# Shared turns of three heads' outputs, and every second mask block copied by ScalarE

## The reference, cut to what matters

```python
Q, K, V = (...)                                # 16 heads of 8 columns each
scores = jnp.einsum('bhqd,bhkd->bhqk', Q, K) / scale
mask = _tpms_mask(L, phase, threshold, temperature)       # one 512 x 512 mask for each head
scores = scores + TPMS_WEIGHT * jnp.log(mask + 1e-06)[None]
attn = jax.nn.softmax(scores, axis=-1)
out = jnp.einsum('bhqk,bhkd->bhqd', attn, V)
out = out.transpose(0, 2, 1, 3).reshape(B, L, H)
return out @ Wo + bo
```

## Time and profile before

| | us |
|---|---|
| median of 3 runs | 875.57 (873.08 to 876.89) |
| the profiled execution | 872.85 |
| its span | 871.0 |
| TensorE busy in the span | 741.7 (85%) |
| ScalarE | 669.0 (77%) |
| VectorE | 569.6 (65%) |
| GpSimd | 192.8 (22%) |

### The profile page before, as it was taken

The page is one execution under the profiler, slowest core; times in us unless marked ns, Lnnn a source line. Parts: engine busy times, 40 slices in busy tenths (PEclk is TensorE's granted clock), DMA queues, the critical chain, the costliest instruction groups (busy, mean ns, idle before and its releaser), DMA issues.

```text
span 871.0 us, 13076 instructions
## 1 busy us (share of the span) xinstructions
PE 741.7 (85%) x4355; PEld 260.3 (30%) x4355; DVE 569.6 (65%) x1464; ACT 669.0 (77%) x799; POOL 192.8 (22%) x167
## 2 busy tenths in 40 slices
PE   0575808999998999999999999999999998999844
PEld 0142401333233323333332233223322332331234
DVE  8968885757989746899783565985423458433265
ACT  1567667788887888888888888887888887888711
POOL 0404762003443203164140031441200002000011
PEclk9986856999999999999999999999999999999987
DMA  5539588854666574756857547668676555456101
GB/s 148 124 124 340 199 295 283 284 178 156 201 203 219 184 201 166 194 177 177 249 186 235 175 138 217 195 184 236 199 234 181 172 176 183 145 189 205 38 2 53
DMA packets 56166, 162.11 MB, mean 186 GB/s; under 512 B 14210, under 2 KB 24594, under 8 KB 45674
## 3 DMA queue, kind: packets, MB, share of 16 engines
q1 hardware_dynamic: 51740, 154.36, 57.8%
q0 software_dynamic: 1904, 5.94, 2.0%
q10 hardware_dynamic: 2446, 0.89, 0.5%
HBM read 117.86 MB, written 43.29 MB: 185 GB/s over the span
## 4 chain that ended last, share of the span: by engine, by line
PE 54%; DVE 22%; ACT 11%; issue 9%; DMA 2%; POOL 1%; SPq 0%; DVEq 0%; POOLq 0%; ACTq 0%
PE S_PS L1656 20%; PE O_PS L1670 18%; ACT BIG L777 9%; PE F_PS L1557 5%; DVE S_PS L1227 5%; PE R_PS L1679 3%; PE F_PS L1552 2%; DVE SC L1064 1%; PE P_PS L1557 1%; PE P_PS L1594 1%; DVE ST L954 1%; DVE XC L1109 1%; DVE BIG L1054 1%; PE P_PS L1598 1%; DMA BIG<-OTS 1%
## 5 line engine op out<-in xcount | busy, mean ns | idle before, releaser
L777 ACT ACTIVATE BIG<-S_PS 128x1024 f32<-128x1024 f32 x512 | 508.7, 1024 | 107.0 <-PE S_PS L1656 104.9
L1656 PE MATMUL S_PS<-BIG 98*128 98x512 bf16 x1024 | 311.1, 389 | 40.1 <-DMA BIG<-OTS 15.4
L1227 DVE COPY S_PS<-BIG 128x512 f32<-128x512 f32 x256 | 159.6, 687 | 178.1 <-ACT BIG L777 175.9
L1670 PE MATMUL O_PS<-BIG,VX 128*9 128x512 f32 x2048 | 269.2, 599 | 1.2 <-ACT OTS L786 1.2
L1656 PEld LDWEIGHTS S_PS<-BIG 98*128 98x128 bf16 x1024 | 79.3, 98 | 294.0 <-ACT BIG L777 138.0
L601 POOL TENSOR_TENSOR XDT<-PART 128x512 bf16<-128x512 f32 x24 | 28.9, 1202 | 293.5 <-ACT PART L742 293.5
L1670 PEld LDWEIGHTS O_PS<-BIG,VX 128*9 128x9 f32 x2048 | 30.8, 88 | 103.3 <-issue 99.1
L578 POOL TENSOR_TENSOR X<-X,BFH 128x512 f32<-128x512 f32 x16 | 24.1, 1528 | 149.8 <-DVE BIG L1054 120.3
L818 ACT ACTIVATE BIG<-S_PS,TEMP 128x1024 f32<-128x1024 f32 x32 | 34.1, 1112 | 21.1 <-PE S_PS L1843 20.7
L578 POOL TENSOR_TENSOR BIG<-BIG,BFH 128x512 f32<-128x512 f32 x16 | 19.9, 1270 | 129.1 <-DVE BIG L1054 111.8
L786 ACT ACTIVATE OTS<-O_PS,CON 128x512 f32<-128x512 f32 x64 | 44.1, 689 | 4.4 <-PE R_PS L1679 4.4
(11 more groups left out here) (197 smaller groups left out, 771.1 us busy)
## 6 DMA issues: line engine op xcount, KB each, us to landing
BIG<-ln_masks SPq DMA_DIRECT2D x62, 1024.0 KB, 6.5
ln_masks<-BIG SPq DMA_DIRECT2D x16, 1024.0 KB, 5.5
BIG<-q_parts SPq DMA_DIRECT2D x63, 192.0 KB
BIG<-k_parts SPq DMA_DIRECT2D x63, 144.0 KB
BIG<-q_parts SPq DMA_DIRECT2D x63, 128.0 KB
q_parts<-PART SPq DMA_DIRECT2D x9, 768.0 KB, 3.8
k_parts<-PART SPq DMA_DIRECT2D x18, 384.0 KB, 4.5
BIG<-k_parts SPq DMA_DIRECT2D x63, 96.0 KB
```

What stands on the lines that cost most here:

```text
L777: act.activation(E[:, m % 2, j, 2 * pair:2 * pair + 2, :], S_PS[:, pair, :, :], ACT.Exp, scale=LOG_WEIGHT)\
L1227: ve.tensor_copy(S_PS[:, pair, i, :], LNM[:, slot, 2 * pair + i, :]).then_inc(s["seeded"], 1)
L1656: mm = pe.matmul(S_PS[:, pair, i, :], KT[0:ALL_ROWS, slot, K_COL[j], 128 * kb:128 * kb + 128], QT[0:ALL_ROWS, slot, j, :], start=False, st ...
L1670: mm = pe.matmul(O_PS[32 * j:32 * j + HD + 1, :], VX[:, slot_of(n), j, kb, h, :], E[:, m % 2, j, kb, :], start=kb == 0, stop=kb == T - 1)
```

## The change

It has two parts.

- Heads are grouped into bunches, by position 0 to 2, 3 to 5, 6 to 8, 9 to 11, 12 and 13, 14 and 15. The outputs of a bunch stand beside each other in O_PS, 9 partitions for each head. The stationary operand of an earlier head is widened to the left, by the value columns that lie before its own, so that its output falls further down; what it writes above is overwritten by the later heads of the bunch. `o_copy`, `turn_o` and `o_norm` run once for a bunch, behind its last head: 24 times instead of 64. The order of the heads in AT becomes the order of work, and the rows of Wo are permuted on the host to fit.
- From head 2 on VectorE copies only the first block of each pair, and ScalarE copies the second, `seed_odd`. On ScalarE it stands behind the exponential of steps 6 and 7, and ahead of the background of that tick. The score products wait for both, and the mask loads too.

```diff
+BUNCHES = ((0, 2), (3, 5), (6, 8), (9, 11), (12, 13), (14, 15))
+NB = len(BUNCHES)
+MOST = max(b - a + 1 for a, b in BUNCHES)
+VPAD = (MOST - 1) * (HD + 1)
+LAST_HEADS = [b for a, b in BUNCHES]
+ROW_BLOCK = {HEAD_ORDER[i]: a + b - i for a, b in BUNCHES for i in range(a, b + 1)}
...
+        def turned_in(m):
+            return bunch_of(m - 2) if m >= 2 and (m - 2) % NH in LAST_HEADS else None
...
             def load_mask(m):
...
-                    sp.wait_ge(s["seeded"], T * (m - 1))
+                    sp.wait_ge(s["seeded"], seeds(m - 1))
+                    if past(odd_seeds(m - 1)):
+                        sp.wait_ge(s["seeded_odd"], odd_seeds(m - 1))
...
+            def seed_odd(m, pair):
+                act.wait_ge(s["e_ready"], STEPS * m - 1 + pair)
+                act.wait_ge(s[f"lnm_in{m % 2}"], 16 * (m // 2))
+                copy(S_PS[:, pair, 1, :], LNM[:, m % 2, 2 * pair + 1, :], "seeded_odd")
...
             def attention(q):
                 for tick in range(TICKS):
                     m, k = q * NH + tick // STEPS, tick % STEPS
-                    if k == 0 and m >= 2:
-                        o_copy(m - 2)
+                    if k == 0 and turned_in(m) is not None:
+                        o_copy(turned_in(m))
                     exp_step(m, k)
+                    if k >= STEPS - 2 and 2 <= m + 1 < NQ * NH:
+                        seed_odd(m + 1, k - STEPS + 2)
...
-            o_copy(NQ * NH - 2)
-            o_copy(NQ * NH - 1)
+            o_copy(NB * NQ - 1)
...
+            ve.memset(VXP[:, :, 0:VPAD], 0.0).then_inc(s["v_pad"], 1)
...
-                for i in range(2):
+                for i in range(2 if m < 2 else 1):
                     ve.tensor_copy(S_PS[:, pair, i, :], LNM[:, slot, 2 * pair + i, :]).then_inc(s["seeded"], 1)
...
-                    if k == 1 and m >= 2:
-                        o_norm(m - 2)
+                    if k == 1 and turned_in(m) is not None:
+                        o_norm(turned_in(m))
...
                     if j == 0:
-                        pe.wait_ge(s["seeded"], T * m + kb + 1)
+                        if m < 2:
+                            pe.wait_ge(s["seeded"], seeds(m) + kb + 1)
+                        elif i == 0:
+                            pe.wait_ge(s["seeded"], seeds(m) + pair + 1)
+                        else:
+                            pe.wait_ge(s["seeded_odd"], odd_seeds(m) + pair + 1)
...
+                ahead = (HD + 1) * (last - m % NH)
...
-                    if past(m):
-                        pe.wait_ge(s["o_copied"], m)
+                    if past(u) and m % NH == first:
+                        pe.wait_ge(s["o_copied"], u)
...
-                    mm = pe.matmul(O_PS[32 * j:32 * j + HD + 1, :], VX[:, slot_of(n), j, kb, h, :],
+                    at = VPAD + ((j * T + kb) * NH + head_of(m)) * (HD + 1)
+                    mm = pe.matmul(O_PS[32 * j:32 * j + ahead + HD + 1, :],
+                                   VXP[:, slot_of(n), at - ahead:at + HD + 1],
                                    E[:, m % 2, j, kb, :], start=kb == 0, stop=kb == T - 1)
...
-                    if k == 1 and m >= 2:
+                    if k == 1 and turned_in(m) is not None:
...
-                        turn_o(m - 2)
+                        turn_o(turned_in(m))
```

More of the change, by code:

```diff
@@ L129, in macaron_kernel @@
         X3 = sb("X3", [128, QB, T, H], F32)
-        VX = sb("VX", [128, 2, QB, T, NH, HD + 1], F32)
+        VXP = sb("VXP", [128, 2, VPAD + QB * T * NH * (HD + 1)], F32)
         PART = sb("PART", [128, 8192], BF16)
@@ L149, in macaron_kernel @@
         SC = sb("SC", [128, 2, 4, QT_, NBLK], F32)
-        RD = sb("RD", [128, T, QB], F32)
+        RD = sb("RD", [128, T, QB, MOST], F32)
         HSEL = sb("HSEL", [128, NH], BF16)
@@ L168, in big @@
             return BIG[:, at:at + size]
+        VX = VXP[:, :, VPAD:].rearrange("p s (j t h d) -> p s j t h d", j=QB, t=T, h=NH)
         E = big(0, 16384).rearrange("p (s j k l) -> p s j k l", s=2, j=QB, k=T)
@@ L243, in macaron_kernel @@
         s = {}
-        for n in """angles_in consts_in zero_set zeros_out ones_set con_set o_zero ident_made vx_ones
+        for n in """angles_in consts_in zero_set zeros_out ones_set con_set o_zero ident_made vx_ones v_pad
                 w_grid w_turned bias_halved
@@ L294, in parts_stored, with bunch_of, bunches_before, seeds @@
                 engine.wait_ge(s["parts_out_k"], K_STORES * n)
+        def bunch_of(m):
+            return m // NH * NB + len([b for b in LAST_HEADS if b < m % NH])
+        def turned_in(m):
+            return bunch_of(m - 2) if m >= 2 and (m - 2) % NH in LAST_HEADS else None
+        def bunches_before(m):
+            return len([i for i in range(max(m, 0)) if i % NH in LAST_HEADS])
+        def seeds(m):
+            return T * min(m, 2) + T // 2 * max(m - 2, 0)
+        def odd_seeds(m):
+            return T // 2 * max(m - 2, 0)
         def stack_name(m):
@@ L778, in exp_step, with o_copy @@
                    .then_inc(s["e_ready"], 1)
-            def o_copy(m):
-                act.wait_ge(s["pv_done"], T * (m + 1))
-                if past(m):
-                    act.wait_ge(s["o_turned"], m)
+            def seed_odd(m, pair):
+                act.wait_ge(s["e_ready"], STEPS * m - 1 + pair)
+                act.wait_ge(s[f"lnm_in{m % 2}"], 16 * (m // 2))
+                copy(S_PS[:, pair, 1, :], LNM[:, m % 2, 2 * pair + 1, :], "seeded_odd")
+            def o_copy(u):
+                act.wait_ge(s["pv_done"], T * (u // NB * NH + LAST_HEADS[u % NB] + 1))
+                if past(u):
+                    act.wait_ge(s["o_turned"], u)
                 else:
@@ L887, in general @@
                         exp_step(n * NH + i, k)
-                    o_copy(n * NH + i)
+                    if i in LAST_HEADS:
+                        o_copy(bunch_of(n * NH + i))
                 for j in range(QB):
@@ L1225, in seed, with o_norm @@
                     ve.wait_ge(s["sigmoids"], 2 * HALF_TILES)
-                for i in range(2):
+                for i in range(2 if m < 2 else 1):
                     ve.tensor_copy(S_PS[:, pair, i, :], LNM[:, slot, 2 * pair + i, :]).then_inc(s["seeded"], 1)
[L1229 to L1232, removed]
+            def o_norm(u):
+                n, (first, last) = u // NB, BUNCHES[u % NB]
+                size = last - first + 1
+                ve.wait_ge(s["o_turned"], u + 1)
+                if u % NB == 0:
                     if not is_short(n):
@@ L1238, in o_norm @@
                         lnm_stored(ve, 13)
[L1239 to L1243, removed]
+                turned = R_PS[:, :].rearrange("p (t g r) -> p t g r", t=T, g=QB)[:, :, :, 0:size * (HD + 1)]\
+                    .rearrange("p t g (s d) -> p t g s d", s=size)
+                ve.reciprocal(RD[:, :, :, 0:size], turned[:, :, :, :, HD]).then_inc(s["o_rd"], 1)
+                ve.wait_ge(s["o_rd"], u + 1)
+                TT(AT[:, slot_of(n), :, :, HD * first:HD * last + HD].rearrange("p j t (s d) -> p t j s d", s=size),
+                   turned[:, :, :, :, 0:HD], RD[:, :, :, 0:size, None].to_broadcast((128, T, QB, size, HD)), ALU.mult)\
                     .then_inc(s["o_normed"], 1)
@@ L1427, in general @@
                           .then_inc(s["seeded"], 1)
-                    o_norm(m)
+                    if h in LAST_HEADS:
+                        o_norm(bunch_of(m))
                 epilogue(n)
@@ L1532, in _ @@
                 attention(q)
-            o_norm(NQ * NH - 2)
-            o_norm(NQ * NH - 1)
+            o_norm(NB * NQ - 1)
             epilogue(NQ - 1)
@@ L1660, in weighted @@
             def weighted(m, kb):
-                n, h = m // NH, head_of(m)
+                n, u = m // NH, bunch_of(m)
+                first, last = BUNCHES[u % NB]
+                ahead = (HD + 1) * (last - m % NH)
                 if kb == 0:
@@ L1683, in turn_at @@
                 g = n * QB + j
-                pe.wait_ge(s["o_normed"], (n + 1) * NH)
+                pe.wait_ge(s["o_normed"], (n + 1) * NB)
                 if is_short(n) and n == NQ - 1:
@@ L1723, in background @@
                 m, k = q * NH + tick // STEPS, tick % STEPS
-                normed = max(m - 2 + (k > 1), 0)
+                normed = bunches_before(m - 2 + (k > 1))
                 if q == 0:
@@ L1827, in general @@
                     pe.wait_ge(s["max_row"], u + 1)
-                    turn_o(m)
+                    if h in LAST_HEADS:
+                        turn_o(bunch_of(m))
                 for j in range(QB):
@@ L1895, in _ @@
                 weighted(last, kb)
-            turn_o(last - 1)
-            turn_o(last)
+            turn_o(bunch_of(last))
             for j in range(0, QB, 2):
@@ L1932 @@
         a = np.ascontiguousarray(inputs[name])
+        if name == "L0_attn_Wo":
+            a = a.reshape(NH, HD, H)[sorted(ROW_BLOCK, key=ROW_BLOCK.get)].reshape(H, H)
```

20 lines of the change are left out of this document (10 added, 10 removed).

## The result

The changed kernel takes 890.96 us, the median of four runs (890.01 to 893.41), against 876.23 us for the kernel before (873.08 to 877.17): 1.017 of its time, 95% interval 1.0143 to 1.0196. It is slower by 14.7 us. The profiled execution took 890.13 us with a span of 888.2 us, 17.2 us longer than the span before.

The account below looks back on a forecast made before the run. Bound: the chain of waits at head changes, through VectorE's four copies and TensorE's pieces. Sum: turns +20, products +2, late changes -7 and -2.5, chains -5, end -1.2, together +6.3 us; forecast 880.5, range 864 to 894.

Parts of the forecast that it names:

- The main rival: VectorE bounds the kernel far more often, from about 15 changes on: faster, 858 to 870 us, chance 0.26.
- seven without a turn: Head changes without a turn where VectorE's first copy starts late: two copies less help in full, -1.0 us each, -7.
- the three with a turn: Head changes with late VectorE that keep a turn: about -0.5 us for two, -1.5 for the last, together -2.5.
- A change without a turn: On-time head change that loses its turn: exponential 2 starts at 5.46 against 5.53 us, worth about zero; 32 such.
- the hand schedule: Start times worked out across a head change, counted from the start of exponential 6, without and with a turn.
- a background product: In 11 changes a product before step 0's scores waits for a delayed ScalarE copy: exponential 2 0.18 later, +2 us.
- A change with a turn: On-time head change keeping its turn: output copy queues behind ScalarE's second odd block, +1.0 us each, +20 for 20.
- the row I took: ScalarE's 128x512 copy out of PSUM, 0.60 us, next exponential 0.47 after its start; 0.48 taken for the new copies.
- the waits in changes without a turn: Argument against ScalarE becoming the bound (about 900 us, chance 0.1): its waits there shrink from 0.96 to below 0.6.
- VectorE's chains behind the change: After late changes VectorE often stays the chain; six heads whose rest gains a further 0.8: -5 us.
- The end: Waits of the last output product and of the copy at 829.92 both go: -0.6 and -0.6 us.
- the bound of the turn: Upper limit for a change that keeps its turn: +1.3 us if the copies cost 0.69; the lower was +0.6.

Follow-up runs that it names:

- The two halves alone: Two runs, each with one part of the change against the kernel before: bunches without ScalarE's mask copies, 870.68 us (0.9938); those copies without bunches, 940.29 us (1.074).
- the reordered copy: Changed kernel, but in changes with a turn ScalarE's output copy stands ahead of its second odd mask block: 873.95 us, 0.9979 of before.
- The experiment with the small additions: Changed kernel, but GpSimd adds the biases to one column of 128 only: 887.38 us, 1.0141 of before.
- the bunches alone: Changed kernel with its bunches, but VectorE makes all four mask copies again: 870.68 us, 0.9938 of before.
- the copies alone: Changed kernel with ScalarE's mask copies, but every head has its own output copy, turn and normalization: 940.29 us, 1.074 of before.
- pair 1 alone: Changed kernel, but ScalarE copies only pair 1's odd block, and only in changes without a turn: 855.97 us, 0.9778 of before.
- pair 1 in every change: Changed kernel, but ScalarE copies only pair 1's odd block, in every change, with the output copy ahead: 856.38 us, 0.9724 of before.

## Why the prediction was right, and which steps failed

**Direction and mechanism: right.** The forecast was slower, by an output copy that queues behind two odd blocks while the turn waits for it. The two halves alone and the reordered copy show exactly this. The size was well short: 880.5 was named, 4.9 us above the median before, and it became 14.7; 890.96 lies just above the 877 to 890 to which the forecast itself gave its chance. The main rival, VectorE as the bound in 15 or more changes, is refuted: where VectorE was late the changes fell as the prediction said (seven without a turn by 8.8, against 7), but there are ten of them. Six of the seven gave 6.0 us, just the 1.0 each of the prediction. The rest, and what the three with a turn gave above their 2.5, is in part luck: the two changes named under the table gave 1.9 and 1.0 us more than their share, and no term of the sum had the clock that they got back.

**A change without a turn: right.** 5.54 measured, 5.46 by the hand schedule. Only one of its copies is on the path, 0.53 to 0.54 from start to start instead of 0.48; the blocks of pair 1 begin at 2.63 instead of 2.60 and the scores of step 1 at 3.38 instead of 3.34, and the pieces behind them take 2.16 instead of 2.12. Behind a background product it takes 6.02 to 6.03 instead of 5.87, so +0.15, against +0.18.

**A change with a turn: mis-sized.** +1.19 measured for +1.0. The output copy starts at 3.17 instead of 3.08, mostly for the two dearer copies ahead of it, and the turn starts 0.25 us after the copy has ended, where I had put 0.04: at 4.09 instead of 3.81. The scores of step 1 start 0.47 behind the turn's start, not 0.61, and exponential 2 2.15 behind theirs, which makes 6.71. The rows held a hint of it: from the end of the output copy (653.77 + 0.69) to the turn (654.73) are 0.27 us. What sets it stays open; behind the last output copy of all, with the same operands, the turn starts after 0.05. The Trainium skill, ScalarE: Activation LUTs, What ACT_TABLE_LOAD costs, gave 0.52 from start to start and so stood nearer to the trace (0.53) than the row I took; by it the sum would have been longer by 2.9 us, an estimate from the same hand schedule (two copies on the path of 20 changes and one on that of 32; the 2.5 of the prediction counts one copy in each of the 62). By the prediction's own numbers the waits in changes without a turn shrink to 0.62, not to below 0.6.

**VectorE's chains behind the change: failed.** I expected -5 us and got +0.1. I had let every chain begin earlier by what VectorE saves and keep its length. Three rests did shrink by 0.70 to 0.71, but one grew by 0.61 and six by 0.15 to 0.25. The experiment with the small additions shows why the largest of these grew: four of its operations stretched by 1.31 us in sum when they ran beside GpSimd. It does not explain the other six: with the small additions they are as long as in the changed kernel, to 0.01 us. Four of them (heads 21 and 37, from 4.50 to 4.71 us, and heads 24 and 40) are at their old length or below it with the bunches alone or the copies alone and at the new one with pair 1 alone, so it takes both halves; why stays open. The step that failed is to move a chain as it is: one that starts earlier can meet other neighbours.

**The end: failed in part.** Both waits went as said: the last output copy starts 3.96 us behind the last exponential instead of 6.00. Of these 2 us only 0.4 reached the end. The products behind them ran at the low one of the clock's two levels, 1.2 GHz, for longer than before. Two stretches at the end of the changed kernel (columns as above):

```profile
858.00:876.00 18.00, 6.47 (x32) 6.02 (x32) 15.92 (x50) 2.08 (x5) 3.19 (x3) 0.65 0.05 18
876.00:880.00 4.00, 4.00 (x19) 3.57 (x18) 0.69 (x2) 0.72 (x2) 0.00 (x0) 0.50 0.19 69
```

TensorE was busy 6.47 of 18 us and at a granted 0.65, and the next 4 us were at 0.50. In the kernel before, the corresponding 4 us (858 to 862) were at 0.57 with TensorE busy for 3.45, and the next at 1.00. That is some 0.5 of the missing 1.6 us; that the low clock took the rest too is not shown.

**What no step had: the clock inside heads.** Two changes with a turn took 8.21 and 8.29 us instead of 6.7. The stretches around the first and the second:

```profile
641.00:645.00 4.00, 1.87 (x12) 0.71 (x8) 1.59 (x3) 3.73 (x6) 0.00 (x0) 0.98 0.83 283
645.00:648.00 3.00, 3.00 (x11) 0.44 (x11) 0.81 (x2) 1.02 (x1) 0.00 (x0) 0.50 1.03 258
...
809.00:812.40 3.40, 1.27 (x9) 0.77 (x8) 1.08 (x2) 3.36 (x5) 0.00 (x0) 0.95 0.68 181
812.40:816.00 3.60, 3.60 (x15) 0.52 (x13) 1.01 (x2) 1.09 (x2) 0.00 (x0) 0.57 0.61 168
```

TensorE had been busy 1.87 of 4.00 and 1.27 of 3.40 us, mostly waiting for the output copy, and was then granted 0.50 and 0.57. Eight output products took 1.91 us there:

```profile
645.34 1.91 PE L1722 MATMUL O_PS<-BIG,VXP 128*18 128x512 f32 x8
```

against 1.05 elsewhere. Together that is 3.1 us that my sum did not have. It is no rule that such a gap does it: six other changes have a gap of 1.54 to 1.63 us ahead of the turn and keep the clock. The clock of the kernel before fell twice too, in the first and the last of its late changes, after TensorE had waited 1.91 us and over 2 us:

```profile
155.20:158.70 3.50, 3.50 (x13) 0.58 (x13) 3.34 (x8) 1.35 (x3) 0.00 (x0) 0.53 0.96 322
...
735.00:739.00 4.00, 3.74 (x16) 1.45 (x16) 4.00 (x6) 1.91 (x2) 0.00 (x0) 0.57 0.35 86
```

So in the net the clock took little: what it took in two changes it gave back, for the most part, in two others. With both blocks on ScalarE and the output copy ahead of the second, TensorE's wait at 0.97, no change fell; with the copies alone five did; with pair 1 in every change two did, one of them right behind a wait of 1.94 us for a DMA. Which changes it hits is not the same from kernel to kernel, and what decides it stays open.

**The range.** 864 to 894 held the time, but near its upper end: the mis-sized turn (+3.8), the missing chains (+5.1), the clock in two changes (+3.1) and the end (+0.8) went one way, and only the products (-2) and the late changes (-2.5) the other; +2.7 more lie at the start and in head 1, where no term stood. The range was wide because it took in half of the first rival on one side and the bound of the turn, 1.3 us, on the other; the turn's 1.19 lay within that bound.

## What to carry to other kernels

Before work is given to an engine that is idle for a sixth of the time (111 of 700 us), look at what is queued behind the place where it is inserted: here two copies of 0.6 us each gained about as much as they cost, and lost 1.2 us wherever a third, on which another engine waits, stood behind them. Share the work that is last on the path (the second pair's blocks) and not what delays the sharing engine's own next step (the first pair's): with the turns shared in both, 39 such copies made the kernel 19 us faster than before and all 124 made it 15 us slower. And where VectorE's work only moves, check which neighbours on GpSimd it will run beside at its new time.

## What the runs showed of the hardware that I had not expected

- A ScalarE copy of 128x512 from SBUF to PSUM took 602 ns, and the next exponential started 0.53 to 0.54 us after its start, not 0.47 as behind a copy out of PSUM.
- Within heads the turn started 0.25 to 0.29 us after the end of the output copy that it waited for (21 of 23 turns of the changed kernel), and behind the last output copy of all 0.05 us.
- Output products with 18 and 27 stationary columns instead of 9 kept their pace: eight took 1.05 us in either; the weight loads grew from 88 to 95 ns in the mean, and quiet changes kept their 5.53 us with the bunches alone.
- A VectorE operation on one column took 0.98 us instead of 0.20 beside GpSimd's additions.
- The granted clock of TensorE fell to its low level for some 3.5 us at a time while heads were scored, in which its mean was 0.98, and not in the same heads from kernel to kernel.
